# Streaming an 8192x8192 float32 matrix through four 4 MB buffers with 32 KB rows instead of sixteen 1 MB buffers with 8 KB rows

## What is computed

```
def reference(x, adj, L0_gnn_u):        # x, u: 8192 x 64, adj: 8192 x 8192, float32
    keep = (u >= 0.1).astype(x.dtype)
    x_drop = x * keep / (1.0 - 0.1)
    z = x + jnp.matmul(adj, x_drop)
    m = jnp.mean(z, axis=-1, keepdims=True)
    v = jnp.var(z, axis=-1, keepdims=True)
    return (z - m) / jnp.sqrt(v + 1e-05)
```

## Time and profile before

| | before |
|---|---|
| runs (3) | 664.34, 664.6, 664.64 us; median 664.6 us |
| profiled execution: span, first to last instruction | 662.4 us |
| profiled execution's own device time | not given apart; the median stands 2.2 us above the span |
| PE busy / PEld busy | 512.4 us (77%) / 150.5 us (23%) |
| DVE / ACT / POOL busy | 54.9 / 17.1 / 0.9 us |
| DMA, mean over the span | 415 GB/s; queue q1 97.4% and q10 2.5% of the 16 DMA engines' time |
| loads of `adj` | 255 of 1 MB, 2 of 512 KB |

### The profile page before, as it was taken

The page is one execution under the profiler, slowest core; times in us unless marked ns, Lnnn a source line. Parts: engine busy times, 40 slices in busy tenths (PEclk is TensorE's granted clock), DMA queues, the critical chain, the costliest instruction groups (busy, mean ns, idle before and its releaser), DMA issues.

```text
span 662.4 us, 5938 instructions
## 1 busy us (share of the span) xinstructions
PE 512.4 (77%) x2304; PEld 150.5 (23%) x2304; DVE 54.9 (8%) x105; ACT 17.1 (3%) x36; POOL 0.9 (0%) x8
## 2 busy tenths in 40 slices
PE   0877778787877878778787887878778787788886
PEld 0222122121211212112122221222122221221443
DVE  2471001010000101001010010101001010010100
ACT  0002000000000000000000000000000000000000
POOL 0000000000000000000000000000000000000000
PEclk9999999999999999999999999999999999999999
DMA  8999999999999999999999999999999999999995
GB/s 344 419 422 420 423 421 422 422 421 422 422 423 423 421 423 422 422 423 423 421 422 424 421 423 422 423 422 422 423 421 423 423 421 423 423 421 422 419 423 225
DMA packets 40617, 274.88 MB, mean 415 GB/s; under 512 B 4512, under 2 KB 6688, under 8 KB 7968
## 3 DMA queue, kind: packets, MB, share of 16 engines
q1 hardware_dynamic: 37008, 268.45, 97.4%
q10 hardware_dynamic: 3600, 6.29, 2.5%
HBM read 272.63 MB, written 2.10 MB: 415 GB/s over the span
## 4 chain that ended last, share of the span: by engine, by line
DMA 65%; SPq 28%; PE 5%; issue 2%; DVE 0%; ACT 0%; DVEq 0%
DMA piece<-adj 57%; SPq L102 28%; DMA piece<-adj_last 8%; PE acc L139 5%; SPq L109 0%; PE folded L154 0%; ACT sums_T L215 0%; ACT std L218 0%; DVE squares L281 0%; DVE y L277 0%; DVE square_sum L284 0%; DVE rows L292 0%; DVE rstd L287 0%; SPq L106 0%; DVEq L291 0%
## 5 line engine op out<-in xcount | busy, mean ns | idle before, releaser
L139 PE MATMUL acc<-piece,xdrop 128*64 128x512 f32 (+1 forms) x2176 | 496.7, 580 | 145.6 <-DMA piece<-adj 120.8
L139 PEld LDWEIGHTS acc<-piece,xdrop 128*64 128x64 f32 x2176 | 134.9, 136 | 494.7 <-DMA piece<-adj 311.7
L277 DVE SCALAR_TENSOR_TENSOR y<-folded,x_sb 128x256 f32<-128x256 f32 (+1 forms) x17 | 7.0, 409 | 573.1 <-PE folded L154 573.1
L215 ACT COPY sums_T<-acc 128x512 f32<-128x512 f32 (+1 forms) x17 | 9.5, 560 | 516.7 <-PE acc L139 516.6
L154 PEld LDWEIGHTS folded<-fold,sums_T 128*128 128x128 f32 x128 | 15.6, 191 | 13.1 <-issue 11.3
L154 PE MATMUL folded<-fold,sums_T 128*128 128x64 f32 x128 | 17.9, 281 | 0.5 <-ACT sums_T L215 0.5
L292 DVE TENSOR_TENSOR rows<-y,rstd 128x256 f32<-128x256 f32 (+1 forms) x17 | 7.0, 410 | 1.6
L281 DVE TENSOR_TENSOR squares<-y 128x256 f32<-128x256 f32 (+1 forms) x17 | 7.0, 409 | 0.6
L284 DVE TENSOR_REDUCE square_sum<-squares 128x4 f32<-128x256 f32 (+1 forms) x17 | 6.9, 404 | 0.6
L218 ACT ACTIVATE std<-square_sum,eps 128x4 f32<-128x4 f32 (+1 forms) x17 | 5.1, 297 | 68.9 <-DVE square_sum L284 68.9
L262 DVE SCALAR_TENSOR_TENSOR u_sb<-u_sb,x_sb 128x1024 f32<-128x1024 f32 x4 | 4.9, 1226 | 23.0 <-DMA u_sb<-u 23.0
(11 more groups left out here) (4 smaller groups left out, 0.4 us busy)
## 6 DMA issues: line engine op xcount, KB each, us to landing
piece<-adj SPq DMA_DIRECT2D x240, 1024.0 KB, 27.1
piece<-adj_last SPq DMA_DIRECT2D x15, 1024.0 KB, 27.4
x_sb<-x ACTq DMA_DIRECT2D x4, 512.0 KB, 16.9
u_sb<-u ACTq DMA_DIRECT2D x4, 512.0 KB, 20.2
out<-rows ACTq DMA_DIRECT2D x15, 128.0 KB, 7.0
piece<-adj_last SPq DMA_DIRECT2D x2, 512.0 KB, 26.0
out<-rows ACTq DMA_DIRECT2D x2, 64.0 KB, 4.8
```

Source lines behind the costliest of these rows:

```text
L139: last = nc.tensor.matmul(acc[i][D * h:D * h + D, 0:cols], xdrop[:, k, :], piece[:, b, :], start=(k < 2), stop=(k >= NB - 2))
L215: nc.scalar.copy(sums_T[:, i, 0:nj * P], acc[i][:, 0:nj * P]).then_inc(sums_copied, 1)
L277: nc.vector.scalar_tensor_tensor(out=y[:, i, 0:nj, :], in0=folded[i][:, 0:nj, :], scalar=1.0 / (1.0 - P_DROP), in1=x_sb[:, bass.ds(block0, ...
```

## The change

Two numbers change, and every size that is worked out of them follows.

```
-SLOTS = 16
+SLOTS = 4
 PB = NB // SLOTS
...
-TAIL_PARTS = (4, 4)
+TAIL_PARTS = (12, 8, 6, 4, 2)
```

## The result

| | before | after |
|---|---|---|
| median of the runs | 664.49 us (664.34 to 664.64, 4 runs) | 656.65 us (656.47 to 658.05, 4 runs) |
| ratio, 95% interval | 1 | 0.9887 [0.9873, 0.9901] |
| profiled execution: span / own time | 662.4 us / not given | 654.8 / 656.78 us |
| q1: packets | 37,008 | 9,792 |
| mean granted TensorE clock | 0.999 | 0.945 |

The change makes the kernel 7.8 us faster; 9.0 were forecast.

What follows compares the result with a forecast made beforehand. The prediction took the stream of DMA transfers, plus what precedes it and follows its last landing, as the bound. -15.4 + 2.5 + 3.9 = -9.0 gave a span of 653.4, with 2.2 for the median 655.6 us; range 651.5 to 667.

Steps and rivals of the forecast that it cites:

- Part 1 (rows): Load stream: rows of 32 KB instead of 8 KB save a fixed 0.010 us per packet, -15.4 us.
- The rival of the stream that runs by bytes: Load stream: 422 GB/s is a ceiling whatever the row, only the losses at both ends count: 671.0 us; chance 0.14.
- the small fixed cost: Load stream: only a third of the 0.010 us belongs to the packet, saving 5.5 us: 665.5 us; chance 0.14.
- Part 2 (start): Start: queues alternate by packet, quarters of x and u take 21.9 us, late reloads leave holes: +2.5 us.
- turns by bytes: Start: queues alternate by bytes, quarters stay 7.5 us apart, no hole: 653 us; chance 0.08 shared with rows cut on the way, mostly this.
- rows cut on the way: Load stream: long rows cut to 8 KB again, gain lost, only the end counts: 668.5 us; shares 0.08 with turns by bytes.
- the forecast's range of 2.0 to 2.6 for slot 2: Start: hole in the stream before slot 2's reload flows, with PE at full or half speed, 2.0 to 2.6 us.
- Part 3 (steady state): Middle: PE takes 7.1 us of every 9.7, the queue never runs dry, stores delay nobody: 0 us.
- The step "after a gap of 1.83 (2.72 on the weight loads) the next group ran in the same 1.94": Middle: products after such a gap kept their time of 1.94 us, so PE's gap growing to 2.6 us costs 0.
- The sign that the prediction named for it, slots of 9 us and more: Middle: PE slots of 9 us and more would show half speed in steady state and the prediction wrong.
- The case had been priced at the end (+5.8 instead of +3.9): End: PE starting at half speed after its gap would make the loss +5.8 us instead of +3.9.
- Part 4 (end): End: PE's backlog ends products 5.1 us after the last landing instead of 1.2, +3.9 us.

Runs made afterwards that it cites:

- `rows_8k`: Changed kernel with each partition's 32 KB in the 60 wide loads stored as four separate 8 KB runs, last chunk kept long: 668.36 us, ratio 1.0063.
- the two kernels with a mended end: Changed kernel with the last but one slot loaded in two parts, 653.59 us; the same with x and u also in line on q1, 651.11 us.
- `last_in_two`: Changed kernel with the last slot in two loads of 16 blocks instead of five: 656.12 us, ratio 0.9881.
- `xu_in_line`: Changed kernel with the quarters of x and u issued by SP on q1, each ahead of its slot's load: 655.65 us, ratio 0.9866.
- `tail_parts`: Changed kernel with the last but one slot loaded in two parts of 16 blocks: 653.59 us, ratio 0.9830.

## Why the prediction was right, point by point

The forecast was 655.6 us, with -9.0 as a sum; measured 656.65 and -7.8.

**Part 1 (rows), -15.4: right in kind, 1.1 us too large.** 16 x (40.05 - 39.16) = 14.3. The fixed cost came out at 0.009 us a packet instead of 0.010; as the text said, it was the difference of two near numbers. Rounding is 0.5 of the 1.1 us: 0.3105 and 0.4706 give 0.0097, and 1536 packets an engine x 0.0097 = 14.9. `rows_8k` shows that it is the row and not the slot. The rival of the stream that runs by bytes falls, and so does the small fixed cost. By the Trainium skill's 3 cycles per packet (DMA: Bandwidth & Descriptors, Why small descriptors are slow) an estimate gives 0.9% of the stream; the chunks became 2.2% shorter, so the trace doesn't agree and the measurement decides. The five parts at the end were put at under 0.1 us. They add 4 rows on each of 8 partitions per engine, and 32 x 0.009 = 0.3 us; the last slot took 10.1 us from the landing before it (634.8) to its own (644.9), where a slot in the middle takes 9.7.

**Part 2 (start), +2.5: right.** The first two quarters 22.0 us apart (forecast 21.9) rule out turns by bytes and rows cut on the way. Putting x and u in line gained 2.05 us at the last but one slot, and 2.5 between the two kernels with a mended end. The 3.0 us missing in 56 to 80 us overstate what that edit can give back, since in line the first 56 us move 406 GB/s instead of 410, which is 0.5 us of stream. How large the hole is hangs on PE's clock, as the forecast's range of 2.0 to 2.6 for slot 2 said. In the profiled execution of `last_in_two`, whose start is the same, slot 2 ran at full speed:

```profile
63.69 20.82 PE L139 MATMUL acc<-piece,xdrop 128*64 128x512 f32 x96 [2.98 <-DVE xdrop L255]
```

```profile
56.00:80.00 24.00, 21.02 (x98) 6.78 (x96) 16.67 (x14) 2.23 (x3) 0.00 (x0) 1.00 0.99 397
```

The run of 96 takes 20.82 us instead of 22.29, the stretch moves 397 GB/s instead of 378, and PE starts on the last but one slot at 633.87, 1.06 us earlier.

**Part 3 (steady state), 0: right in its price, wrong in one reason.** The step "after a gap of 1.83 (2.72 on the weight loads) the next group ran in the same 1.94" was carried over to gaps of 2.6 us behind 7 us of work, and that failed. Of 49 slots between 125 and 605 us 34 take 7.09 us and 15 take 8.46 to 8.78, and the stretches at the start of the slot at 302.06 show why (the clock is the third number from the end):

```profile
302.00:304.00 2.00, 1.94 (x6) 0.68 (x8) 0.00 (x0) 0.00 (x0) 0.00 (x0) 0.60 0.84 360
304.00:306.00 2.00, 2.00 (x8) 0.53 (x6) 0.00 (x0) 0.00 (x0) 0.00 (x0) 0.54 1.10 475
306.00:308.00 2.00, 2.00 (x12) 0.67 (x10) 0.00 (x0) 0.00 (x0) 0.00 (x0) 1.00 1.03 442
```

After a gap of 2.62 us the granted clock is at its lower level, 1.2 GHz, for most of 4 us, then back at 2.4. The mean fell from 0.999 to 0.945. Of the 28 slots that follow a gap of 2.6 us or more, 14 began at half speed in this way. It cost nothing in the middle, because 8.8 us are still under the beat of 9.7. The sign that the prediction named for it, slots of 9 us and more, was set just too high to catch it. The case had been priced at the end (+5.8 instead of +3.9), though only as an aside.

**Part 4 (end), +3.9: right in mechanism, and its full speed was luck.** It is 14.8 us from the landing of the last but one slot to the last product, as forecast. The term itself is 3.6: PE ends 4.9 us behind the last landing (forecast 5.1), because the short rows of the five parts made that landing later, and ended 1.3 behind it before. The last but one slot follows a gap of 2.67 us. Behind such gaps half of the slots began at half speed, so the 7.1 us that the forecast put for it, with the row that failed in part 3 as its reason, came by luck; `xu_in_line` met the other case. `tail_parts` gave 3.1 back, and `last_in_two` shows that the five parts are hidden.

**Sum.** The last landing came 656.0 - 644.9 = 11.1 us earlier: -14.3 in the beat, 0.3 for the short rows of the five parts, and the 2.9 that are left over for the start (forecast 2.5; 1.06 less in the profiled execution of `last_in_two`). With +3.6 at the end that is -7.5, against 7.6 between the two profiled spans and -7.8 between the medians. The forecast's -9.0 was too large by what part 1 had too much; the start, 0.4 too small, and the end, 0.3 too large, nearly cancel.

**What stays open.** One of the four runs of the changed kernel took 658.05 us, 1.3 to 1.6 above the others, one of `last_in_two` 657.74, and one of `tail_parts` 651.93, 1.6 below its next. A slot at the other speed, the last but one or slot 2 of the start, is worth 1.1 to 1.7 us and would be enough; there is no profile of those runs, so it isn't shown. Which slots come out at half speed differs between executions, and the runs don't settle by what.

## What to carry to other kernels

When a kernel is bound by its loads, ask what one packet costs beyond its bytes: two row sizes in one trace are enough for a line. Here it forecast the time of a third to 0.2%, but the saving, a difference, only to 7%. Larger pieces are paid for where the pipeline fills and drains, so price three places apart: the beat, the first pieces (what shares the queues and takes turns by packet with a row eight times as long?), and the work left behind the last landing. Then treat only the ends and keep the long rows in the middle: here the small loads of the start went onto the queue of the large ones, ahead of the slots that need them, and the last but one piece was cut in two. That took 656.65 to 651.11 us. Fewer and larger buffers also lengthen the compute engine's gaps, and that slack is used up at once when only two are left.

## What was not expected of the hardware

- TensorE lost its full clock behind gaps of 2.6 us that followed 7 us of work: from 100 to 600 us the mean granted clock was 0.95. With gaps of 1.25 us (8 slots) and of 0.55 us (16) it was 1.00 there, and with gaps of mostly 3 to 8 us (2 slots) 0.91.
- A row of 64 KB was one packet: 6,624 packets on q1 with 2 slots are 46 loads, those of x and u included, times 144. It lasted 2.418 us, 0.008 less than two of 32 KB.
- Output stores with rows of 1 KB took 14.0 us to land instead of 7.0; 12 had been forecast. It goes by the rows that they share the engines with: 7.1 us beside rows of 8 KB in slots of 4 MB (`rows_8k`), 9.3 beside 16 KB, 23.5 beside 64 KB. No wait in the traces names them.
